# One graph layer on one Trainium2 core: key rows by broadcast, earlier scores and output products, norms ahead of splits, x loaded ahead of the weights

## What is computed

```python
xn = layernorm(x)                                         # (384, 1024)
q, k, v = xn @ wq.T + bq, xn @ wk.T + bk, xn @ wv.T + bv
q2, k2, v2 = q @ wiq.T + biq, k @ wik.T + bik, v @ wiv.T + biv    # 16 heads of 64
mask = full((384, 384), -inf); mask[src, dst] = softplus(etw)[type - 1]   # the last edge of a pair counts
mask[i, i] = softplus(etw)[3] where no edge stands there
attn = softmax(q2 @ k2.T / 8 + mask)
gnn = (attn @ v2) @ wo.T + bo
qf, kf = elu(xn @ mq.T) + 1, elu(xn @ mk.T) + 1           # the mixer, 16 heads
mix = (qf @ (kf.T @ (xn @ mv.T))) / (qf @ sum(kf) + 1e-6) @ mo.T + mbo
x = x + gnn + mix
gate = top4(sigmoid(layernorm(x) @ expert_sel.T))         # 4 of 32 experts for each node
out = x + sum over e of (relu(layernorm(x) @ keys[e]) * gate[:, e]) @ values[e]
```

## Time and profile before

| what | value |
|---|---|
| median of 3 runs | 960.46 us (959.93 to 962.93) |
| the profiled execution | 962.8 us, its span 960.6 us |
| TensorE (PE) busy | 887.3 us, 92% |
| VectorE (DVE) busy | 663.0 us, 69% |
| ScalarE (ACT) busy | 530.2 us, 55% |
| GpSimd (POOL) busy | 335.1 us, 35% |
| moved by DMA | 203 MB, mean 211 GB/s |

### The profile page before, as it was taken

How to read it: one execution, slowest core, us unless ns; L and a number is a source line. 1 busy time by engine, 2 the same in 40 slices (tenths; PEclk the granted TensorE clock), 3 DMA queues, 4 the chain that set the end, 5 groups by cost and what they waited for, 6 DMA issues and landing times.

```text
span 960.6 us, 13957 instructions
## 1 busy us (share of the span) xinstructions
PE 887.3 (92%) x4482; PEld 749.9 (78%) x4482; DVE 663.0 (69%) x1050; ACT 530.2 (55%) x686; POOL 335.1 (35%) x292
## 2 busy tenths in 40 slices
PE   2789999999999999898984899999999999999993
PEld 2788889988989999644774788878888888888882
DVE  6676766653343544567387599979888899988880
ACT  3244421242322422467232388878888888888870
POOL 0703444454442000299101113433334344443331
PEclk9999999999999999999995699999999999999997
DMA  7423332223335333200282499999999999999941
GB/s 305 167 88 138 132 132 89 88 90 131 132 133 181 118 109 124 88 1 1 88 321 117 161 327 362 363 319 355 358 362 367 365 364 366 364 358 365 365 138 21
DMA packets 40453, 203.00 MB, mean 211 GB/s; under 512 B 12880, under 2 KB 13136, under 8 KB 18400
## 3 DMA queue, kind: packets, MB, share of 16 engines
q1 hardware_dynamic: 26496, 186.66, 51.8%
q0 software_dynamic: 13200, 15.03, 6.4%
q10 hardware_dynamic: 720, 0.83, 0.2%
HBM read 203.33 MB, written 21.15 MB: 234 GB/s over the span
## 4 chain that ended last, share of the span: by engine, by line
PE 67%; DMA 13%; POOL 7%; DVE 7%; issue 2%; ACT 2%; ACTq 0%; POOLq 0%; DVEq 0%; SPq 0%
PE ps L1103 20%; PE ps L1105 20%; PE ps L1104 20%; POOL pr L389 6%; DMA out_dram<-ysb,pcol 3%; DMA xg<-xt_dram,gcol 2%; DMA raw_x<-in_values 2%; DMA raw_x<-in_keys 2%; DMA out_dram<-etmp,pcol 2%; PE ps L1286 2%; PE ps L1133 1%; PE ps L1217 1%; PE ps L1292 1%; DMA c_all<-in_c_all 1%; POOL out_dram L574 1%
## 5 line engine op out<-in xcount | busy, mean ns | idle before, releaser
L632 ACT ACTIVATE wh<-raw 128x1024 fp32r<-128x1024 f32 x88 | 93.1, 1061 | 253.0 <-PE ps L1105 242.2
L788 DVE TENSOR_TENSOR wl<-raw,wh 128x1024 fp32r<-128x1024 f32 x88 | 110.7, 1263 | 156.8 <-ACT wh L632 156.4
L547 POOL DMA_INDIRECT plane<-code,idx x96 | 101.1, 1053 | 124.0 <-DMA plane<-code,idx 86.3
L1103 PE MATMUL ps<-wh_x,hTh 128*128 128x512 f32 x248 | 103.3, 416 | 0.0
L1103 PE MATMUL ps<-wh,xgTh 128*128 128x512 f32 x248 | 98.2, 396 | 0.0
L1105 PE MATMUL ps<-wh_x,hTl 128*128 128x512 f32 x248 | 98.2, 396 | 0.0
L1104 PE MATMUL ps<-wl,xgTh 128*128 128x512 f32 x248 | 97.9, 395 | 0.0
L1105 PE MATMUL ps<-wh,xgTl 128*128 128x512 f32 x248 | 97.8, 394 | 0.0
L1104 PE MATMUL ps<-wl_x,hTh 128*128 128x512 f32 x248 | 97.6, 393 | 0.0
L389 POOL TENSOR_SCALAR pr<-pr,mx 128x384 f32<-128x384 f32 x48 | 58.7, 1238 | 100.9 <-DVE mx L358 100.9
L1103 PE MATMUL ps<-xnh,wh 128*128 128x384 f32 x256 | 87.5, 342 | 2.7 <-issue 2.7
(11 more groups left out here) (221 smaller groups left out, 2031.2 us busy)
## 6 DMA issues: line engine op xcount, KB each, us to landing
raw<-in_keys SPq DMA_DIRECT2D x34, 1024.0 KB, 11.4
raw_x<-in_values SPq DMA_DIRECT2D x34, 1024.0 KB, 12.3
raw_x<-in_keys SPq DMA_DIRECT2D x30, 1024.0 KB, 12.2
raw<-in_values SPq DMA_DIRECT2D x30, 1024.0 KB, 12.5
raw<-in_w_v SPq DMA_DIRECT2D x8, 1024.0 KB, 4.8
raw<-in_w_q SPq DMA_DIRECT2D x8, 1024.0 KB, 4.9
raw<-in_w_k SPq DMA_DIRECT2D x8, 1024.0 KB, 4.8
raw<-in_w_mq SPq DMA_DIRECT2D x4, 1024.0 KB, 7.8
```

The source lines that it names most:

```text
L547: nc.gpsimd.indirect_dma_start(plane[m], bass.IndirectOffsetOnAxis(idx[:, g:g + 1].bitcast(U32), 0), code[:, g:g + 1], None, bounds_check= ...
L632: nc.scalar.activation(wh[:, s % SUB], raw[:, c % RAW, 2 * (s % 2):2 * (s % 2) + 2, :], ACT.Copy)\
L788: nc.vector.tensor_tensor(wl[:, s % SUB], raw[:, (s // 2) % RAW, 2 * (s % 2):2 * (s % 2) + 2, :], wh[:, s % SUB].bitcast(F32), ALU.subtrac ...
L1103: nc.tensor.matmul(o, ah, bh_, start=start, stop=False)
```

## The change

1. **Opening.** SP waits for x's second tile instead of all constants. ACT loads the identity and the edges first and the rest once x is there. VectorE makes the keys after the first tile's statistics.
2. **Key rows.** TensorE transposes the keys once (96 x 128), ScalarE copies them, GpSimd writes them to DRAM (`key_dram`) and loads each group of 16 columns back as a row of 2048 broadcast to all partitions (`rows_of_keys`, six loads of 1 MB, three buffers that lie where `pT` comes later). The `dup` jobs are gone from the list, and the halves of the projections alternate between the bank sets. VectorE does four compares after each split from `mk0`'s first on (`same_keys`). ScalarE waits for the last before it evacuates `v0`.
3. **Planes.** Both are filled from one tile by six transfers; the diagonal is written by three indirect ones. The two output biases are added to each other first: four GpSimd sums instead of six.
4. **Attention.** The scores of the first four units stand ahead of `k21`'s last quarter, with their masks and the first reciprocal. Every sixth unit is normalised by ScalarE. `o0`'s last splits stand in step 8, the first four expert splits at the end of attention, and `o0`'s products in four pieces between the last transposes and values.
5. **Routing.** Other PSUM banks for transposes and logits; VectorE's copy of the last transpose stands ahead of `choose(0)`; ScalarE makes `slot1h_h` and `lane1h` tile by tile; `slot1h` stands directly behind `gidx`; the first gathered x is split in two halves, and four expert splits stand behind it.

```diff
-    names = ["xT0", "xT1", "mq0", "dup0", "mq1", "dup1", "mk0", "dup2", "mk1", "dup3", "mv0", "dup4",
-             "mv1", "dup5", "lin", "v0", "mix0", "mix1", "mix2", "v1", "mT0", "mT1", "mo0", "mo1",
+    names = ["xT0", "xT1", "mq0", "mq1", "mk0", "mk1", "mv0", "mv1", "lin", "v0", "mix0", "mix1", "mix2", "v1", "mT0", "mT1", "mo0", "mo1",
@@ sync @@
-            sp.wait_ge(s_const, 16 * N_CONST)
+            sp.wait_ge(s_x[NT - 2], 16)
...
-                if c == RAW - 1:
+                if c == RAW + 1:
@@ gpsimd @@
+            def rows_of_keys(k):
+                g = GROUP * GROUPS[k]
+                pool.dma_start(key_rows[k % 3][:, :], key_dram[g * P:(g + GROUP) * P, :].rearrange("e o -> o e").to_broadcast([P, GROUP * P]))\
+                    .then_inc(s_rowk[k % 3], 16)
+            pool.wait_ge(s_keyc, 1)
+            pool.dma_start(key_dram.rearrange("(g p) o -> g (p o)", p=P), key_t[0:EC, :]).then_inc(s_keyd, 16)
+            pool.wait_ge(s_keyd, 16)
+            for k in range(3):
+                rows_of_keys(k)
...
+            pool.wait_ge(s_idx, 1)
+            rows_of_keys(3)
             pool.wait_ge(s_rows, 16 * N_ROWS)
             pool.wait_ge(s_xn, NT)
...
+            nc.gpsimd.tensor_tensor(mbo_b[:, :], mbo_b[:, :], bo_b[:, :], ALU.add).then_inc(s_pch, 1)
...
+            pool.wait_ge(s_idx, 2)
+            rows_of_keys(4)
             for k in range(0, len(GROUPS), 2):
                 pool.wait_ge(s_idx, k + 2)
@@ vector, split @@
+                    if s >= jobs["mq1"]["sub_end"]:
+                        for u in range(units[0], min(units[0] + (2 if s == jobs["mk0"]["sub_end"] else 1), 4 * len(GROUPS))):
+                            same_keys(u)
+                            units[0] += 1
@@ vector, same_keys @@
+                for q in range(4 * c, 4 * c + 4):
+                    g = GROUP * GROUPS[k] + q
+                    link(nc.vector.scalar_tensor_tensor(junk[:, :], key_rows[k % 3][:, q * P:(q + 1) * P], ef[:, 3, g:g + 1],
+                                                        after[:, :], ALU.is_equal, ALU.mult, accum_out=dup[:, g:g + 1]))
@@ attention, TensorE @@
-            for i in range(STEPS + 5):
-                if i < STEPS:
-                    scores(i)
-                if 0 <= i - 4 < STEPS and (i - 4) % NT == NT - 1:
-                    values_of((i - 4) // NT)
-                if 0 <= i - 3 < STEPS:
+            for i in range(STEPS + 3):
+                if EARLY // 2 <= i < STEPS:
+                    scores(pe, i)
+                if i == 3:
+                    pe.wait_ge(s_free, att_free + EARLY)
+                if i >= 3:
                     turn(2 * (i - 3))
                     turn(2 * (i - 3) + 1)
+                if i == STEPS:
+                    values_of(PAIRS - 2)
+                if i < STEPS and i >= 4 and (i - 4) % NT == NT - 1:
+                    values_of((i - 4) // NT)
+                if i == STEPS:
+                    out_part(0, 1)
+                if i == STEPS + 1:
+                    out_part(1, 2)
+            out_part(2, 4)
+            values_of(PAIRS - 1)
+            out_part(4, DC)
@@ attention, ScalarE @@
+                if 0 <= i - 1 < STEPS and normed_by_act(2 * i - 1):
+                    normed(2 * i - 1)
+                if i == SPLIT_STEP:
+                    split_out()
+                if i - 4 == STEPS - 1:
+                    act.wait_ge(s_t, 2 * STEPS)
+                    split_ahead()
@@ scalar @@
+                        if name == "v0" and b == 0:
+                            act.wait_ge(s_idx, len(GROUPS))
```

367 lines of the change are left out of this document (225 added, 142 removed).

## The result

The changed kernel takes **927.82 us** (median of 4 runs, 926.38 to 928.80) against 960.81 for the kernel before in the same session; ratio 0.9652, 95% interval 0.9632 to 0.9673. The forecast was 926, with a range of 918 to 938. The profiled span fell from 960.6 to 925.4 us, by 35.2, where the sum said 34.9. Three of the terms behind that sum were wrong by 2 to 5 us, in both directions.

A forecast was written before the change was run, and what follows sets the result against it. TensorE, busy for 92% of the span, was taken as the bound. Opening 23.4, attention and output projection 3.1 and routing 8.4 summed to 34.9 us off 960.5, giving 926 us, range 918 to 938.

The forecast's parts named there:

- First product 17.3, gain 4.2: Opening: weights start earlier and splits leave the path, so the first projection product comes at 17.3 instead of 21.50 us.
- 96 transposes 12.3: Opening: the six groups of 16 transposes for the duplicate test go from TensorE, gaining 12.3 us.
- bank waits 9.2: Opening: projection halves alternate between PSUM bank sets, so TensorE's waits of 4.9 and 4.3 us go, gaining 9.2.
- (a): Opening: VectorE's compares and splits are slowed beside GpSimd's bias sums, delaying mk1's split; cost 1 us (0 to 11).
- (b): Opening, between mv1 and lin: lin waits for VectorE's split, four compares and three evacuations; cost 2 us (1 to 3).
- (c): Opening: ScalarE waits for the last of the duplicate test before v0's first evacuation; cost 1 us (0 to 3).
- Rival 1: VectorE falls behind in the opening; 10 us of the sums reach TensorE whole, giving 936 us; chance 0.2.
- The middle keeps its 7.59 period, for GpSimd was not its limit: Attention: values groups stay 7.59 us apart because TensorE is the bound; ScalarE's share of the normalising buys nothing there.
- Cost of the scatter 0: Scatter of the 96 edge columns starts later but ends near 295 us, still covered before its use at about 310.
- Routing 8.4: From the output projection's end to the first expert product: a shorter chain (5.2) plus the clock gain 8.4 us.
- rival 2: TensorE's clock stays down in routing, 3.2 us more, giving 929 us; chance 0.15.
- Expert stage 0: Expert stage, from the first expert product to the end: its loop is unchanged, so costed at nothing.

The follow-up runs named there:

- the warming: Changed kernel with 28 transposes of the identity into an unused bank while TensorE waits for the norms; 927.83 us.
- the last experiment: Changed kernel with sums first, 28 dummy transposes, first choice earlier, ScalarE zeroing, gather ahead of scatter, landing wait behind the next gather; 917.52 us.

## Why the prediction came out right, point by point

- **First product 17.3, gain 4.2: wrong, 20.17.** The step "It loses about 1 us because x lands with less beside it" failed. x's last tile did land about 1 us earlier, but the keys that the change puts ahead of the last four statistics, with their wait for the edges, used that up: the last statistics ended at 10.5 us in both. And "then one transpose" took for granted that the transposes keep pace with the rows; at 0.205 us each they were the limit, which the warming showed (17.90). The half clock behind the first product, 1.3 us before, is gone, as only the upper end of that term had it; with it the gain is 2.6.
- **96 transposes 12.3, bank waits 9.2, half clock behind them 1.7: right.** None of the three is left: 1.3 + 1.3 + 12.3 + 9.2 + 1.7 less the waits of 1.3 and 1.9 is 22.6, and 22.5 are seen at lin.
- **Costs (a) 1, (b) 2: right,** 1.3 and 1.9. **(c) 1: too small,** 1.8, of which 1.2 is the wait for v0's evacuation; the wait of 0.7 behind it was there before (0.6). Rival 1 is out: the sums met small instructions and cost one quarter's split, not 10 us. Opening 20.7 instead of 23.4. (The "lin at about 121" of the prediction's last part did not follow from its own sum, which gives 123.)
- **"The middle keeps its 7.59 period, for GpSimd was not its limit": wrong,** and the costliest step. The comparison of 7.59 with 7.34 was of two rates; it did not ask when GpSimd's last unit ends, and GpSimd had no pause in 58.7 us. It also overlooked that the diff moves the value products behind the turns. The prediction's own sign of being wrong, a period below 7.2, came true. Stretch k21 to o1: 7.5 us gained without the moved scores. The forecast was 3.1, though its terms add up to 3.0. Of the 7.5, 3.5 are ScalarE's help in the new order and 2.3 the early scores (2.0 forecast), each measured by taking it away from the whole; the remaining 1.7 (1 forecast) is by difference, for order and output products less the two splits. The two splits alone cost 0.9 and not 2, for the period that holds them is 7.91 us long. The values came 8.3 us after k21 (9.0).
- **Cost of the scatter 0: right, by 0.3 us.** Its forecast end was 9 us too early.
- **Routing 8.4: right in sum,** 9.9. The 8.4 is 5.2 and the 3.2 of rival 2 for the clock. No row of the kernel before shows the 3.2; the runs show 3.1 over the first logits and 1.7 more over the last, which ran at full clock too. The gate product waits 1.03 instead of 3.06, as forecast. Not foreseen: GpSimd's zeroing now beside VectorE, 1.0 against. Rival 2 (clock down) is what the moved-back splits bring about. The last 16 logits are a matter of luck: in five of the nine other changed kernels with the splits in the new place they take 3.6 us instead of 1.94, and in one of these the first 32 take 4.6.
- **Expert stage 0: wrong,** 2.9 lost. The loop is unchanged, but its phase is not: the first scatter is issued in 6.93 us instead of 1.64, and TensorE waits 5.7 us for gathered rows instead of 2.5. With the last experiment's order no such wait is left.

The sum was right because -2.7 in the opening and -2.9 in the expert stage met +4.4 in attention and +1.5 in routing. The range would have held either half of these errors alone (920 or 931 us); the single number owes it to luck.

## What to carry to other kernels

An engine that works without a pause through a stretch bounds its end even where the loop beside it has a longer period: look at the end of its block, not at the rate alone, and remove both bounds or expect nothing from one. Before moving a transfer ahead of another in an in-order queue, write down its round with the landings: what overlapped a landing before may stand in a row with it after. And the clock is a term of its own: in routing four splits in another place were worth 7.2 us, and slower logits alone made 4.8 of the loss without them.

## What the runs showed of the hardware that I had not expected

- TensorE's first 24 transposes ran at 0.205 us each and, after 28 dummies at 0.21, at 0.117, while the profile's granted clock read 1.00 for both. At the start of a program the time of one instruction tells more than that row.
- GpSimd's scatter took 6.8 to 6.9 us to issue beside VectorE's splits, which have two inputs in SBUF and have no pause, and 1.6 where one pause came first; where at most three operations in a row overlapped it, it took 1.6 to 2.6. The Trainium skill (SBUF — State Buffer, Who interferes with whom) has a two-input tensor_tensor take only the read side of the shared port pair, which would leave writing descriptors free, an inference by its own words. The rows do not decide it: the scatter also reads its row numbers (`pcol`) from SBUF, which may be what was held up, and no run here took the splits away from beside it.
- GpSimd's memset, which reads nothing, stretched VectorE's operations on 12 numbers from 0.17 to 0.55, 0.88 and 0.81 us; with ScalarE zeroing, or with the zeroing at another time, they were at 0.17 again.
